# Another prelude and a spread feed-forward preparation in a fused attention and expert kernel

## The reference

```python
xn = layernorm(x)                                  # x: (2, 1024, 128)
# attention, 16 heads, two 64-wide queries and keys for each head
A1, A2 = Q1 @ K1.T * s, Q2 @ K2.T * s
O = (softmax(A1) - lam * softmax(A2)) @ V
Y = layernorm(concat(O) @ Wo + bo) * gamma + beta
attn = Y * 0.2
# feed-forward: the routing looks at the mean token of each batch entry
main = gelu(xn @ W1m + b1m) @ W2m + b2m
probs = softmax(mean(xn, axis=1) @ w_gate + b_gate)
top_vals, top_idx = top_k(probs, 2)
gate_w = top_vals / sum(top_vals)
expert_out = sum_k gate_w[k] * (gelu(xn @ W1e[k] + b1e[k]) @ W2e[k] + b2e[k])
ffn = a * main + (1 - a) * expert_out              # a = clip(alpha, 0.1, 1)
out = x + attn + ffn
```

## Time and profile before

| what | value |
|---|---|
| median of 3 runs | 1227.66 us (1227.1 to 1227.86) |
| profiled execution, its own time | 1227.46 us |
| span of the profiled execution | 1225.6 us |
| busy in the span: PE, DVE, ACT, POOL | 96%, 74%, 79%, 83% |
| mean granted clock of PE | 0.987 of full speed |
| chain that ended last: PE, POOL, DVE | 85%, 9%, 4% |

### The profile page before, as it was taken

The page is one execution under the profiler, slowest core; times in us unless marked ns, Lnnn a source line. Parts: engine busy times, 40 slices in busy tenths (PEclk is TensorE's granted clock), DMA queues, the critical chain, the costliest instruction groups (busy, mean ns, idle before and its releaser), DMA issues.

```text
span 1225.6 us, 28035 instructions
## 1 busy us (share of the span) xinstructions
PE 1171.1 (96%) x9730; PEld 842.1 (69%) x9730; DVE 910.6 (74%) x1537; ACT 967.8 (79%) x1709; POOL 1016.5 (83%) x654
## 2 busy tenths in 40 slices
PE   2887999999999999999999999999999999998998
PEld 2655677776676767767777776676777767765798
DVE  6975688877878787788878877878787788884510
ACT  2285698888989888889898888989888889885432
POOL 3099989999999999999999999999999999989100
PEclk9998899999999999999999999999999999997999
DMA  6952012111111111111111111111111111110000
GB/s 139 328 118 49 9 47 49 48 48 44 48 48 48 48 48 48 48 40 33 31 47 48 48 48 43 48 48 48 48 48 48 48 40 32 27 43 1 1 18 18
DMA packets 74118, 63.41 MB, mean 52 GB/s; under 512 B 45156, under 2 KB 63076, under 8 KB 74084
## 3 DMA queue, kind: packets, MB, share of 16 engines
q1 hardware_dynamic: 73076, 62.78, 20.1%
q10 hardware_dynamic: 880, 0.19, 0.1%
q0 software_dynamic: 128, 0.01, 0.0%
HBM read 19.96 MB, written 9.44 MB: 24 GB/s over the span
## 4 chain that ended last, share of the span: by engine, by line
PE 85%; POOL 9%; DVE 4%; ACT 1%; issue 1%; DMA 0%; DVEq 0%; ACTq 0%; POOLq 0%
PE ps L481 27%; PE ps L497 20%; PE ps L511 18%; PE ps L435 8%; PE ps L523 5%; POOL p_mix L392 4%; PE ps L575 3%; PE ps L562 2%; POOL work L389 2%; PE ps L463 1%; POOL w L376 1%; DVE pt L805 1%; POOL x_all L371 0%; DVE small L849 0%; DMA x_all<-in_L_attn_X 0%
## 5 line engine op out<-in xcount | busy, mean ns | idle before, releaser
L849 DVE TENSOR_REDUCE small<-ps 128x1 f32<-128x1024 f32 x512 | 613.8, 1220 | 123.5 <-PE ps L481 122.6
L392 POOL TENSOR_TENSOR p_mix<-p_mix,work 128x1024 f32<-128x1024 f32 x256 | 609.6, 2381 | 21.4
L497 PEld LDWEIGHTS ps<-ident,p_mix 64*128 64x128 f32 x4096 | 309.6, 139 | 199.7 <-issue 176.4
L683 ACT ACTIVATE pt<-ps 128x512 f32<-128x512 f32 x512 | 305.8, 597 | 142.1 <-PE ps L497 132.5
L497 PE MATMUL ps<-ident,p_mix 64*128 64x64 f32 x4096 | 353.2, 227 | 22.5 <-POOL p_mix L392 18.0
L389 POOL TENSOR_SCALAR work<-work,small 128x1024 f32<-128x1024 f32 x256 | 308.3, 1204 | 66.5 <-DVE small L874 66.5
L670 ACT ACTIVATE p_mix<-ps,small 128x1024 f32<-128x1024 f32 x256 | 285.1, 1114 | 18.0 <-DVE small L849 17.9
L670 ACT ACTIVATE work<-ps,small 128x1024 f32<-128x1024 f32 x256 | 284.6, 1112 | 12.9 <-DVE small L849 8.6
L511 PE MATMUL ps<-pt,v_h 128*64 128x512 f32 x1024 | 249.0, 607 | 0.0
L481 PE MATMUL ps<-k_hi,q_hi 64*128 64x512 f32 x512 | 234.7, 458 | 3.7 <-ACT p_mix L670 1.7
L481 PE MATMUL ps<-k_hi,qx_hi 64*128 64x512 f32 x512 | 230.9, 451 | 0.0
(11 more groups left out here) (133 smaller groups left out, 1306.7 us busy)
## 6 DMA issues: line engine op xcount, KB each, us to landing
qx_hi<-q_hi SPq DMA_DIRECT2D x64, 256.0 KB, 3.8
qx_lo<-q_lo SPq DMA_DIRECT2D x64, 256.0 KB, 4.3
v_scratch<-pt SPq DMA_DIRECT2D x16, 512.0 KB, 3.5
v_h<-v_scratch SPq DMA_DIRECT2D x32, 256.0 KB, 2.9
wqk_raw<-in_L_attn_Wk SPq DMA_DIRECT2D x31, 64.0 KB, 1.8
wqk_raw<-in_L_attn_Wq SPq DMA_DIRECT2D x31, 64.0 KB, 1.9
x_all<-in_L_attn_X SPq DMA_DIRECT2D x2, 512.0 KB, 4.9
wo_dup<-in_L_attn_Wo SPq DMA_DIRECT2D x2, 512.0 KB, 8.7
```

Of the source, the lines that this page charges most:

```text
L392: pool.tensor_tensor(e1, e1, e2, ALU.add).then_inc(mix_done, 1)
L497: mm = pe.transpose(pt_ps[:, c * D:(c + 1) * D], p_mix[rows, col:col + P], ident[rows, rows])
L683: act.activation(pt4[:, kb % 2, :, j * P + half * D:j * P + (half + 1) * D], pt_ps.rearrange("p (c q) -> p c q", c=KC), ACT.Copy).then_inc ...
L849: dve.tensor_reduce(neg_max[:, m:m + 1], slot[SLOT[k, s]], AX.X, ALU.max, negate=True)\
```

## The change

There are three parts.

- **Prelude.** The statistics are made with `bn_stats` and `bn_aggr`, one instruction for each tile of 128 columns, and one `tensor_scalar` for each tile normalises it straight from the input. The input of b = 0 arrives as two transfers of four tiles. PE's transposes start after four normalised tiles, go to other PSUM banks (6, 7, 2, 3), and the low parts of b = 0 stand on DVE in the middle of the statistics of b = 1. ACT, not POOL, now rounds the first head's weights and the V weights. Its weight transfers are issued ahead of the bias transfers. PE's first projection waits for each half of x separately. The routing's product stands after V unit 13 instead of 9, and the two groups of routing instructions on DVE after 12 and 20 moved units instead of 8 and 16.
- **Shared part of the preparation.** What does not need the experts (`set_main`: the 0.2 on gamma and beta, the main net's bias and second weights, and adding that row to all 16 input tiles) runs on POOL in the prelude, after the routing's last step and before POOL's first mix.
- **Expert part.** `set_expert(n)` gives POOL at most one such instruction in a step, over steps 20 to 61. The second weights of the four experts are scaled in halves of 256 columns, the input tiles get their bias row in halves of 512 columns.

```diff
-SET_STEPS = 3 + 2 * SETS + 4 * B
+SET_MAIN = 5 + B
+SET_STEPS = SET_MAIN + 1 + 2 * (SETS - 1) + B + 2 * B + (SETS - 1)
+COEF_AT, BIAS_AT, SUM_AT, ADD_AT = 20, (21, 22, 25, 26), (28, 29), (33, 36, 41, 44)
+W2_AT = (49, 50, 52, 53, 57, 58, 60, 61)
...
+            def set_main():
+                pool.wait_ge(route, 14)
                 pool.tensor_copy(coef[:, 0:1], a_mix).then_inc(set_step, 1)
-                pool.wait_ge(set_step, 2)
                 pool.tensor_scalar(gb_bc[:, 0:2 * E], gb_bc[:, 0:2 * E], OUT_SCALE, None, ALU.mult)\
                     .then_inc(set_step, 1)
-                pool.wait_ge(experts_loaded, 64 * SETS)
-                for s_ in range(SETS):
+                pool.wait_ge(main_loaded, 64)
+                pool.wait_ge(set_step, 1)
+                pool.tensor_scalar(bias[:, 0, :], bias[:, 0, :], coef[:, 0:1], None, ALU.mult).then_inc(set_step, 1)
+                pool.tensor_scalar(w2[:, 0:HC * E], w2[:, 0:HC * E], coef[:, 0:1], None, ALU.mult)\
+                    .then_inc(set_step, 1)
+                pool.wait_ge(set_step, 3)
+                pool.tensor_tensor(bias[:, 0, :], bias[:, 0, :], gb_bc[:, E:2 * E], ALU.add).then_inc(set_step, 1)
+                pool.wait_ge(set_step, 5)
+                pool.wait_ge(xn_ready, 2 * B)
+                for b in range(B):
+                    add_row(bias[:, 0, :], b * TB, (b + 1) * TB)
...
+            def set_expert(n):
+                if n == COEF_AT:
+                    pool.wait_ge(gates_in, 16)
+                    pool.wait_ge(experts_loaded, 64 * (SETS - 1))
+                    pool.wait_ge(route, 14)
+                    pool.tensor_scalar(coef[:, 1:SETS], gates, a_rest, None, ALU.mult).then_inc(set_step, 1)
...
             pool.wait_ge(id_ready, 4)
-            split_w(0)
+            pool.wait_ge(w_loaded, 48)
+            pool.tensor_tensor(wqk_raw[:, 3 * D:], wqk_raw[:, 3 * D:], eighth.to_broadcast([P, P]), ALU.mult)\
+                .then_inc(w_split, 1)
+            pool.wait_ge(w_split, 2)
+            pool.tensor_tensor(wqk_lo[:, :], wqk_raw[:, :], wqk_hi[:, :].bitcast(F32), ALU.subtract)\
+                .then_inc(w_split, 1)
+            pool.wait_ge(wv_split, 1)
+            pool.tensor_tensor(wv_lo, wv_raw, wv_hi.bitcast(F32), ALU.subtract).then_inc(wv_split, 1)
             start_y()
             split_w(1)
+            set_main()
...
-                if isinstance(g, int) and g == 0:
-                    if k == 6:
-                        set_weights()
-                    if 7 <= k < 7 + B:
-                        add_biases(k - 7)
-                    if 7 + B <= k < 7 + B + SETS:
-                        scale_w2(k - 7 - B)
+                set_expert(n)
...
+            sqrt_var(0)
+            act.wait_ge(w_split, 1)
+            act.activation(wqk_hi[:, :], wqk_raw[:, :], ACT.Copy).then_inc(w_split, 1)
+            high_x(0)
+            high_x(1)
+            act.wait_ge(wv_loaded, 16)
+            act.activation(wv_hi, wv_raw, ACT.Copy).then_inc(wv_split, 1)
+            sqrt_var(1)
...
+            def stats(t0, t1):
+                for t in range(t0, t1):
+                    last = dve.bn_stats(parts[:, t, :], x3[:, t, :])
+                return last
+            def moments_of(b):
+                dve.wait_ge(ln_step, 7 * b + 1)
+                for t in range(b * TB, (b + 1) * TB):
+                    last = dve.bn_aggr(moments[:, t, :], parts[:, t, :])
...
+            def normalise(b):
+                dve.wait_ge(sqrt_done, b + 1)
+                inv_std(slice(b * TB, (b + 1) * TB), ln_step, 7 * b + 3)
+                dve.wait_ge(ln_step, 7 * b + 7)
+                for t in range(b * TB, (b + 1) * TB):
+                    norm = dve.tensor_scalar(xn3[:, t, :], x3[:, t, :], moments[:, t, 0:1], rstd_x[:, t:t + 1],
+                                             ALU.subtract, ALU.mult)
+                    if t % 4 == 3:
+                        norm.then_inc(xn_ready, 1)
```

More of the change, by code:

```diff
@@ L130, in build @@
         o_ps = ps[:, 7 * BANK:8 * BANK]
-        x_loaded = [sem(f"x_loaded{b}") for b in range(B)]
-        small_loaded, bias_loaded = sem("small_loaded"), sem("bias_loaded")
+        x_loaded = [sem(f"x_loaded{i}") for i in range(3)]
+        small_loaded, bias_loaded, rows_loaded = sem("small_loaded"), sem("bias_loaded"), sem("rows_loaded")
         wv_loaded, wo_loaded, experts_loaded = sem("wv_loaded"), sem("wo_loaded"), sem("experts_loaded")
+        main_loaded = sem("main_loaded")
         id_ready, ln_step, sqrt_done = sem("id_ready"), sem("ln_step"), sem("sqrt_done")
@@ L196, in slot_free, with xt_bank @@
             return exp_done, 2 * (g * BODY + k) + what + 1
+        def xt_bank(i):
+            bank = (6, 7, 2, 3)[i]
+            return ps[:, bank * BANK:(bank + 1) * BANK]
         block = ctx.enter_context(nc.Block())
@@ new lines, in set_main, with add_row @@
+                pool.tensor_tensor(bias[:, 0, :], bias[:, 0, :], gb_bc[:, E:2 * E], ALU.add).then_inc(set_step, 1)
[3 more added lines that the diff above has]
+                    add_row(bias[:, 0, :], b * TB, (b + 1) * TB)
+            def add_row(row, t0, t1):
+                xb = x3[:, t0:t1, :]
+                pool.tensor_tensor(xb, xb, row.unsqueeze(1).to_broadcast([P, t1 - t0, E]), ALU.add)\
+                    .then_inc(set_step, 1)
@@ L374, in scale_w2 @@
-            def scale_w2(s_):
-                part = w2[:, s_ * HC * E:(s_ + 1) * HC * E]
-                pool.tensor_scalar(part, part, coef[:, s_:s_ + 1], None, ALU.mult).then_inc(set_step, 1)
-            pool.wait_ge(id_ready, 4)
-            split_w(0)
+                if n in SUM_AT:
+                    first = 1 + TOPK * SUM_AT.index(n)
+                    pool.wait_ge(set_step, SET_MAIN + SETS)
+                    pool.tensor_tensor(bias[:, first, :], bias[:, first, :], bias[:, first + 1, :], ALU.add)\
+                        .then_inc(set_step, 1)
@@ new lines, in set_expert @@
+                if n in ADD_AT:
+                    part = ADD_AT.index(n)
+                    pool.wait_ge(set_step, SET_MAIN + SETS + B)
+                    add_row(bias[:, 1 + TOPK * (part // 2), :], part * TB // 2, (part + 1) * TB // 2)
+                if n in W2_AT:
+                    part = W2_AT.index(n)
+                    cols = slice((2 + part) * HC * E // 2, (3 + part) * HC * E // 2)
+                    s_ = 1 + part // 2
+                    pool.tensor_scalar(w2[:, cols], w2[:, cols], coef[:, s_:s_ + 1], None, ALU.mult)\
+                        .then_inc(set_step, 1)
@@ L433, in proj @@
                     for half in range(2):
+                        if isinstance(n, int) and n == 0 and j != 1:
+                            pe.wait_ge((xt_hi, xt_hi, xt_lo)[j], half + 1)
                         col = half * D if w else 3 * D
@@ L606, in _ @@
         def _(act):
+            for col, src, cols in ((P + D, Wq, P), (0, Wk, P), (P, Wk, D)):
+                act.dma_start(wqk_raw[:, col:col + cols], src[0, :, 0:cols]).then_inc(w_loaded, 16)
             act.dma_start(bq_in, bq).then_inc(bias_loaded, 16)
@@ L733, in _ @@
             xn3 = p_mix[:, 0:2 * S].rearrange("p (t e) -> p t e", e=E)
-            sq3 = work[:, 0:S].rearrange("p (t e) -> p t e", e=E)
+            parts = work[:, 0:6 * NT].rearrange("p (t v) -> p t v", v=6)
+            moments = small[:, 0:2 * NT].rearrange("p (t v) -> p t v", v=2)
             def inv_std(t, s, base):
@@ new lines, in stats @@
+            def stats(t0, t1):
[6 more added lines that the diff above has]
+                    last = dve.bn_aggr(moments[:, t, :], parts[:, t, :])
+                last.then_inc(ln_step, 1)
+                dve.wait_ge(ln_step, 7 * b + 2)
+                dve.tensor_scalar(var_x[:, b * TB:(b + 1) * TB], moments[:, b * TB:(b + 1) * TB, 1],
+                                  LN_EPS, None, ALU.add).then_inc(ln_step, 1)
@@ L781, in low_part @@
+            dve.wait_ge(x_loaded[0], 16)
+            stats(0, TB // 2)
+            dve.wait_ge(x_loaded[1], 16)
+            stats(TB // 2, TB).then_inc(ln_step, 1)
+            moments_of(0)
+            normalise(0)
+            dve.wait_ge(x_loaded[2], 16)
+            stats(TB, TB + TB // 2)
+            low_x(0)
+            low_x(1)
+            stats(TB + TB // 2, NT).then_inc(ln_step, 1)
+            moments_of(1)
+            normalise(1)
             def low_part(n, par, w, tile):
```

106 lines of the change are left out of this document (32 added, 74 removed).

## The result

The changed kernel takes 1210.83 us (median of 4 runs, 1207.32 to 1214.13), the one before 1227.76 in the same series: a ratio of 0.9854, 95% interval 0.9828 to 0.988. The forecast was 1205.4 in a range of 1198 to 1214. The profiled execution took 1207.97 us with a span of 1206.2, so 19.4 us less span than before. The four runs lie in two groups, near 1207.6 us at mean granted clocks of 0.990 and 0.992 and near 1213.9 at 0.984 and 0.986, and the forecast's sum is compared with the profiled execution, which belongs to the first.

A forecast was written before the change was run, and what follows sets the result against it. The prediction saw a prelude, an early attention held up by POOL and a long PE-bound stretch. 1227.46 - 10.8 - 20.0 + 8.5 = 1205.2, plus 0.2 for the median: 1205.4 us, range 1198 to 1214.

The forecast's parts named there:

- What bounds: Whole kernel: prelude, early attention held up by POOL, then a long stretch PE fills, whose work the change leaves untouched.
- The early block: Steps 8 to 24: preparation on POOL makes PE wait and halves its clock; removing this gains 20.0 us.
- The shared part: Before POOL's first mix: set_main, 8.8 us with waits, fits POOL's idle time with 4.6 us to spare; costs nothing.
- The spread: Steps 20 to 61: 15.9 us of expert pieces on POOL, partly hidden by its idle time; PE waits 8.5 us.
- spread and clock: Rival, steps 20 to 61: nothing hidden, half clock after two waits of some 2 us; 10.2 us more, 1216; chance 0.12.
- The prelude: Before attention: DVE's shorter chain brings the first V move at 22.3 instead of 33.14, gaining 10.8 us.
- late end: Prelude: first V move at 25.5 us with dear small operations and both POOL hits on DVE.
- blocked prelude: Rival, prelude: four POOL operations each hold DVE once, 5.6 us instead of 1.3; total 1210; chance 0.11.
- Fully hidden: Rival, attention: the spread expert pieces cost PE nothing, 8.5 us less than forecast; total 1197; chance 0.14.
- No bite: Rival, early attention: POOL's lateness has another origin, so the 20.0 us loss stays; total 1225; chance 0.03.
- slower: Rival, attention: all 15.9 us exposed and 24 us lost to low clock in six groups; total 1237; chance 0.02.

The follow-up runs named there:

- idle-slot kernel: Changed kernel with the expert pieces only in steps with n mod 8 = 3 or 4, over steps 11 to 131: 1200.61 us, ratio 0.9797.
- the last version: Changed kernel plus expert pieces in POOL's idle steps, two POOL operations moved later, 22 extra PE transposes before those of b = 1: 1199.45 us.

## Why the prediction was right

The forecast of 1205.4 stands against 1207.97 for the profiled execution and 1210.83 for the median. The terms were not all as close as the sum: the prelude gave 3.1 us less than forecast and the spread cost 0.9 less, and these two partly cancel. By its own steps:

- **What bounds.** Right. From step 80 to the end 824.8 us before and 825.0 after, and the stretch of PE's work was only shifted.
- **The early block, 20.0.** Right in size and cause: 19.69 between steps 8 and 24, and the same with the old prelude (66.07 for 16 steps).
- **The shared part, 0.** Right. Expected from 36.7 to 45.5 with a cover of 4.6; measured 39.97 to 48.37, with 4.85 of idling before the first mix. It moved with the prelude and kept its cover.
- **The spread, 8.5.** Right in mechanism and near in size: 7.64 between steps 24 and 80, 6.23 of it waits. Seven waits in the named places, foreseen as 0.2, 1.0, 0.7, 1.2, 1.2, 2.1 and 2.1, measured as 0.33, 0.85, 0.60, 0.85, 1.03, 1.91 and 0.99, together 6.56. The dip of the clock behind the 1.91 cost the other 1.4. The rest of the miss is the last wait, 0.99 where 2.1 was foreseen. The remark against the rival "spread and clock" offers a reason: PE slowed by the dip gives POOL its lead back. That isn't shown. All eight profiled executions with the wait of 1.9 had the dip behind it, and where it lasted twice as long, the last wait was 1.04. The prices of POOL's pieces, bounded by rows only, hold: 0.92 for half a weight tile and 1.30 for 512 columns against the 0.9 and 1.3 taken.
- **The prelude, 10.8.** This is the term that was mis-sized: 7.66. Four things lie between. (Its late end, 25.5, is 25.2 by its own terms: 21.0 + 1.6 + 2.6.)
  - The normalisations were taken at 0.2 each and cost about 0.26, 2.1 us for eight where nothing held them: 0.5 more for each batch entry, 0.9 together. That is inside the ends of 0.15 and 0.3 taken from the reduction over 1024 columns, as the statistic is (0.22).
  - POOL hit DVE three times, where half of two hits was assumed: 0.88 for one tile of line 819 instead of 0.33, 1.21 for line 810 and 1.32 for line 783, where both cost 0.17 in their free form. 2.7 us, 1.3 assumed: 1.4 more. The first of them was in none of the forecast's terms but in the rival "blocked prelude". When POOL's two later operations were moved away, their two hits were gone and the first V move came at 22.21, where the forecast had 22.3 with half of the hits in it.
  - The low parts of x, 4.3 us assumed with what stands beside them, took 4.0: 0.3 less.
  - The V stage took 22.84 us instead of 21.7. PE had stood still for 2.70 us and ran at half clock from 19 to 25.8. This item belongs to the one execution: the second profile of the same program, with a pause of 2.68, has its clock back at full earlier and a V stage of 21.83.
  The two together, first V move 2.0 late and V stage 1.1, are the 3.1 that are missing. By the second profile (first score 46.51) 2.5 are missing, all of them before the first V move (24.68).
- **The rivals.** "Blocked prelude" was partly right: three of its four hits are there, 2.7 us instead of its 5.6, and the fourth, under POOL's multiplication of 128 columns, cost 0.25 us in the idle-slot kernel's trace (line 788 took 0.42 instead of 0.17 at 7.81). The prediction had cited the Trainium skill, "SBUF — State Buffer", section "Who interferes with whom", by which normalisations with `tensor_scalar` can be blocked as well as operations with two inputs in SBUF. The trace agrees: a normalisation (line 819) and a small `tensor_scalar` (line 810) were held, of which no row of before had spoken, as well as the two-input operation of line 783. "Fully hidden" is refuted for this table and shown for another: the same pieces in the idle slots cost nothing. "Spread and clock" had the dip behind a wait of about 2 us right, but most of the work was hidden: 6.2 us of waits for 16 us of work. "No bite" and "slower" are refuted.
- **The range.** 1198 to 1214 held the median and, but for 0.13 us, the slowest run. The scatter of 6 us was not foreseen. It widens the interval of the ratio and is no part of any step. The median lies above the 1201 to 1210 that the prediction gave for its own mechanism: with the scatter, it is inside the stated range by the range's width.

What stays open: where the executions 6 us above the others lose their time. The changed kernel's second profile, 3.3 us longer than the first, loses it in longer and additional stretches at half clock, but none of the longest executions has a profile. Their mean clocks would be enough: between 0.990 at 1207.97 us and 0.984 at 1214.13 lie, by an estimate from these shares, some 7 us of full clock. Kernels with waits of PE near 1.9 us had such runs more often, yet the last version, whose longest wait for the add is 0.73, had two in six.

## What to carry over

Work that is moved off a busy place has to land where its engine idles, not merely be cut small: find the idle slots of the steady loop in the trace, and put no more there than they hold. Here the same 16 us of work cost 7.6 us with one table and nothing with another. And when a chain of tiny DVE operations sets the end, look at which long GpSimd operation starts just before each of them, and start it after the chain or make it wait: two lines of order brought the first V move forward by 1.4 to 2.5 us, though the scatter of the runs hides this in the medians. And profile the same program twice before giving a cause to a microsecond: the two profiles of the changed kernel differ by 3.3 us.

## What the runs showed of the hardware

- A DVE operation on 8 columns takes 0.17 us alone and 1.21 or 1.32 us beside a GpSimd operation, ending with it. It holds for a `tensor_scalar` with one tensor input as for a `tensor_tensor` with two, and a `tensor_scalar` on 128x128 took 0.88 instead of 0.33. `bn_aggr` and a reciprocal on 8 columns kept their length beside the same GpSimd operations.
- `bn_stats` over 128 columns takes 0.22 us in a row of four, `bn_aggr` 0.08 and a `tensor_scalar` on 128x128 0.27 in a row of eight.
- TensorE's clock, in the 14 profiled executions: it was at half behind PE's pause in the new prelude in all five executions where the pause was 2.25 to 2.92 us long, and not behind one of 1.47. Behind the wait of 1.83 or 1.84 us for the V weights it was at half in one of three, the one in which PE had stood still for 1.51 us before. Behind the waits of 1.89 to 1.98 us in step 58 it was at half in eight of eight. Behind PE's first wait for an add, 0.73 to 0.75 us and present in every execution, it was at half in five of 14, the second profile of the changed kernel among them and the first not. So the same wait in the same program doesn't fix the clock behind it.
- One program on one core scatters: the changed kernel took 1207.32 to 1214.13 us in four runs, the kernel before 1225.4 to 1233.7 in one series of eleven.
